# Panel loads out of attention, two panels summed in the first layer, s1 rows in four pieces, value products on VectorE

## What is computed

```python
seq = (x @ W_seq).reshape(2048, 16, 32)
s1, s2 = einsum('nhd,d->hn', seq, a1), einsum('nhd,d->hn', seq, a2)
scores = leaky_relu(s1[:, :, None] + s2[:, None, :], 0.2) + (1 - adj) * -65500.0
hidden = einsum('hij,jhd->ihd', softmax(scores), seq).reshape(2048, 512)
x = layernorm(x + elu(hidden @ W_out + b_out))
A = (adj + adj.T) * 0.5 + I
A = dinv[:, None] * A * dinv[None, :]         # dinv = rowsum(A) ** -0.5
x = layernorm(x + (adj @ A) @ x)               # adj stands for Coefficient2
```

## Time and profile before

| | us |
|---|---|
| runs shown | 787.64, 788.12, 789.85 (median 788.12) |
| the profiled execution, its own time | 786.61 |
| span of its instructions | 784.8 |
| PE busy | 749.7 (96%) |
| DVE busy | 554.7 (71%) |
| ACT busy | 409.9 (52%) |
| POOL busy | 130.1 (17%) |
| mean share of full TensorE clock granted | 0.992 |

### The profile page before, as it was taken

One profiled execution on the slowest core, in us unless ns is written; L12 is line 12 of the kernel. 1 busy time (PEld: TensorE's weight loads), 2 busy tenths in 40 slices (PEclk: granted clock), 3 DMA queues, 4 the chain that ended last, 5 costly groups with the idle time before them and its releaser, 6 DMA issues.

```text
span 784.8 us, 29353 instructions
## 1 busy us (share of the span) xinstructions
PE 749.7 (96%) x13731; PEld 552.4 (70%) x13731; DVE 554.7 (71%) x799; ACT 409.9 (52%) x302; POOL 130.1 (17%) x142
## 2 busy tenths in 40 slices
PE   6999799988999999999999999999999999999997
PEld 2444699988999999999999999444434444444443
DVE  2887899998988999999999983687772211333233
ACT  2874887986977888788897880333321111000000
POOL 0000113012320211101111001364433100000000
PEclk9999799999999999999999999999999999999999
DMA  7992510255313111011110121599119800001111
GB/s 304 413 406 103 235 57 5 84 110 110 56 60 84 58 58 36 26 58 58 58 58 4 58 71 31 97 186 175 54 31 172 119 0 1 18 36 41 41 40 41
DMA packets 17770, 71.65 MB, mean 91 GB/s; under 512 B 2016, under 2 KB 2016, under 8 KB 13408
## 3 DMA queue, kind: packets, MB, share of 16 engines
q1 hardware_dynamic: 13040, 52.99, 17.7%
q0 software_dynamic: 4608, 16.78, 14.1%
HBM read 77.89 MB, written 8.65 MB: 110 GB/s over the span
## 4 chain that ended last, share of the span: by engine, by line
PE 78%; DVE 15%; issue 5%; ACT 1%; DMA 1%; POOL 0%; DVEq 0%; POOLq 0%; SPq 0%; ACTq 0%
PE bank L631 13%; PE bank L534 12%; PE bank L533 12%; PE bank L531 11%; PE bank L618 11%; PE bank L467 7%; PE bank L579 7%; DVE RZ L852 5%; PE bank L587 3%; DVE RG L871 2%; DVE RG L867 2%; DVE RP L816 1%; PE bank L571 1%; DVE MT L892 1%; DMA RZ<-in_L_gnn_W_seq_dram 1%
## 5 line engine op out<-in xcount | busy, mean ns | idle before, releaser
L531 PE MATMUL bank<-RP,RG 128*128 128x66 f16 x4096 | 388.8, 193 | 6.9 <-DVE RG L871 3.6
L534 PE MATMUL bank<-RP,MT 128*128 128x66 f16 x4096 | 388.7, 194 | 3.6 <-issue 3.6
L531 PEld LDWEIGHTS bank<-RP,RG 128*128 128x128 fp8e4 x4096 | 386.3, 98 | 8.3 <-DVE RG L871 3.6
L533 PE MATMUL bank<-RP,RG 128*128 128x66 f16 x4096 | 388.7, 195 | 2.1 <-issue 2.1
L534 PEld LDWEIGHTS bank<-RP,MT 128*128 128x128 fp8e4 x4096 | 386.4, 98 | 3.2 <-issue 3.2
L533 PEld LDWEIGHTS bank<-RP,RG 128*128 128x128 fp8e4 x4096 | 386.4, 97 | 2.7 <-issue 2.7
L689 ACT ACTIVATE RZ<-RZ,TAB 128x2048 int8<-128x2048 f32 x160 | 306.6, 1988 | 15.3 <-DVE RG L867 14.5
L852 DVE TENSOR_SCALAR RZ<-RZ,TAB 128x2048 int8<-128x2048 f32 x96 | 132.3, 1378 | 0.0
L867 DVE TENSOR_TENSOR RG<-RZ,MT 128x512 int32<-128x512 int32 x160 | 121.7, 760 | 0.1
L631 PE MATMUL bank<-RZ,MT 128*128 128x512 f16 x512 | 110.7, 379 | 2.2 <-DVE MT L1023 2.2
L391 POOL TENSOR_TENSOR RP<-SEQ,TAB 128x528 f32<-128x528 f32 x32 | 52.2, 1652 | 331.8 <-DVE RP L818 256.7
(11 more groups left out here) (103 smaller groups left out, 593.2 us busy)
## 6 DMA issues: line engine op xcount, KB each, us to landing
RG<-in_adj_t_dram SPq DMA_DIRECT2D x16, 1024.0 KB, 10.6
RZ<-s_rows_dram SPq DMA_DIRECT2D x16, 1024.0 KB, 5.8
seq_copy_dram<-SEQ SPq DMA_DIRECT2D x1, 4224.0 KB, 14.2
S2Q<-in_adj_p_dram POOLq DMA_DIRECT2D x8, 512.0 KB, 6.3
S2Q<-in_adj_tp_dram POOLq DMA_DIRECT2D x8, 512.0 KB, 11.3
RZ<-in_x_dram SPq DMA_DIRECT2D x16, 256.0 KB, 3.5
RP<-in_adj_p_dram POOLq DMA_DIRECT2D x8, 512.0 KB, 7.1
RP<-in_adj_tp_dram POOLq DMA_DIRECT2D x8, 512.0 KB, 13.8
```

The lines of the kernel that those rows point to most:

```text
L531: mm(pb[bank][:, c:c + 2 * DV], step, high, start=(j == 0 and i % IB == 0), stop=(j == NT - 1), skip_group_check=True)
L533: mm(pb[bank][:, c:c + 2 * DV], step, low, start=False, stop=(j == NT - 1), skip_group_check=True)
L534: last = mm(pb[bank][:, c + DV:c + 3 * DV], mask, edge, start=False, stop=(j == NT - 1), skip_group_check=True)
```

## The change

- POOL loads no panel during attention. `NE = 2`: panels 0 and 1 are loaded once PE has used all but two slots of the last head, and added at once. The others up to 9 are loaded and added in the loop of the first layer, diagonals three iterations behind. `y_part` sums two panels; `y_product` does 14 instead of 12. Panels 10 to 15 are loaded, added and completed one y_product at a time.
- `NS = 4`: a row of s1 is loaded in four pieces, each behind another quarter of the G tiles of the head before; the readers wait for all four. SP's loop over heads is unrolled.
- `prep` moves to DVE, ahead of `low_operands(0)` for head 0 and at j = 4 of head h for head h+1; its wait for `pn_ready` falls.
- `o_product` 0 and 1 do column tiles 0 to 14 first and the last one of both after that. `take_back(t)` goes ahead of `low_z(t)`.

```diff
--- before.py
+++ after.py
@@ -42,6 +42,8 @@
     CLAMP = 20.0
     NG = 16
     NQ = 4
+    NE = 2
+    NS = 4
     NP = 6
     LAG = 5
     NZ = 4
@@ -54,7 +56,7 @@
     ACTZ = [j for j in range(NT) if j not in OWN]
     NA = 4
     GT = 4
-    AT_EVAC, AT_HIGH, AT_LOW, AT_HID = 7, 8, 11, 13
+    AT_PREP, AT_EVAC, AT_HIGH, AT_LOW, AT_HID = 4, 7, 8, 11, 13
     assert CW * IB <= 512 and 2 * NB == 8
     ctx = ExitStack()
@@ -316,21 +318,23 @@
             sp.dma_start(s1_rows[:, :], s1T).then_inc(s1_stored, 16)
             sp.wait_ge(s1_stored, 16)
-            def load_s1(h, u):
-                sp.dma_start(S1B[:, u, :], s1_rows[DS(h, 1), :].broadcast_to([P, N])).then_inc(s1b_in[u], 16)
+            def load_s1(h, q):
+                i = slice(q * (N // NS), (q + 1) * (N // NS))
+                sp.dma_start(S1B[:, h % 2, i], s1_rows[h:h + 1, i].broadcast_to([P, N // NS])).then_inc(s1b_in[h % 2], 16)
             sp.wait_ge(seq_ps, NT)
-            load_s1(0, 0)
-            load_s1(1, 1)
+            for q in range(NS):
+                load_s1(0, q)
+            for q in range(NS):
+                load_s1(1, q)
             sp.wait_ge(tabs_done, 1)
             sp.dma_start(seq_copy[:, :], SEQ[:, :, :, :].rearrange("p t h d -> p (t h d)")).then_inc(seq_stored, 16)
-            with sp.Fori(1, H // 2) as p:
-                for u in range(2):
-                    h = p * 2 + u
-                    sp.wait_ge(z_ready, h * NV - NV)
-                    sp.wait_ge(g_ready, h * NT - NT)
-                    load_s1(h, u)
+            for h in range(2, H):
+                sp.wait_ge(z_ready, (h - 1) * NV)
+                for q in range(NS):
+                    sp.wait_ge(g_ready, (h - 1) * NT + q * (NT // NS))
+                    load_s1(h, q)
             sp.wait_ge(z_ready, (H - 1) * NV)
             sp.wait_ge(g_ready, (H - 1) * NT)
@@ -383,18 +387,6 @@
                 gp.affine_select(out=m[:, :], in_=m[:, :], compare_op=ALU.not_equal, fill=one, base=0,
                                  pattern=[[-1, P]], channel_multiplier=1).then_inc(consts, 1)
-            def prep(h):
-
-                if h >= 1:
-                    gp.wait_ge(pn_ready, h)
-                for e, tab in enumerate((EE, FF)):
-                    gp.tensor_tensor(V2[:, :, e, :], SEQ[:, :, h, :], tab[:, h, :].unsqueeze(2).broadcast_to([P, NT, DV]),
-                                     ALU.mult).then_inc(v2_ready, 1)
-
-            gp.wait_ge(tabs_done, 1)
-            prep(0)
-            prep(1)
-
             gp.wait_ge(deg_done, 1)
             gp.tensor_tensor(DINV[:, :], DINV[:, :], mhalf[:, :], ALU.pow).then_inc(pow_done, 1)
@@ -410,15 +402,6 @@
                 diag = panel(t)[:, t, :]
                 gp.tensor_tensor(diag, diag, id2[:, :], ALU.add).then_inc(s2_done, 1)
-            for h in range(2, H):
-                prep(h)
-                if 3 <= h < 3 + NQ:
-                    load_panel(h - 3)
-                if 4 <= h < 4 + NQ:
-                    add_panel(h - 4)
-                if 5 <= h < 5 + NQ:
-                    add_diagonal(h - 5)
-
             def x_minus_1(t):
                 gp.wait_ge(xr_in[t % 2], (t // 2) * 16 + 16)
                 gp.tensor_tensor(xr[:, t % 2, :], xr[:, t % 2, :], mone[:, :].broadcast_to([P, D]), ALU.add).then_inc(xm_done, 1)
@@ -430,24 +413,32 @@
             x_minus_1(0)
             x_minus_1(1)
+            gp.wait_ge(g_used, NG + H * NT - 2)
+            for t in range(NE):
+                load_panel(t)
+            for t in range(NE):
+                add_panel(t)
             gp.wait_ge(att_end, 1)
             for t in range(NT):
-                if t < NP:
-                    load_panel(NQ + t)
-                if 2 <= t < 2 + NP:
-                    add_panel(NQ + t - 2)
-                if 4 <= t < 4 + NP:
-                    add_diagonal(NQ + t - 4)
+                if t + NE < NQ + NP:
+                    load_panel(t + NE)
+                if NE <= t < NQ + NP:
+                    add_panel(t)
+                if 2 <= t < 2 + NE:
+                    add_diagonal(t - 2)
+                if 3 + NE <= t < 3 + NQ + NP:
+                    add_diagonal(t - 3)
                 rstd_of(t, var_done, rstd_done)
                 if t + 2 < NT:
                     x_minus_1(t + 2)
-            for t in range(NQ + NP, NT):
-                gp.wait_ge(y_ps, NQ if t < 2 * NQ + NP else t - NQ - NP + 1)
-                load_panel(t)
-            for t in range(NQ + NP, NT):
-                add_panel(t)
-            for t in range(NQ + NP, NT):
-                add_diagonal(t)
+            for t in range(NQ + NP, NT + 2):
+                if t < NT:
+                    gp.wait_ge(y_ps, t - NQ - NP + 1)
+                    load_panel(t)
+                if NQ + NP < t <= NT:
+                    add_panel(t - 1)
+                if NQ + NP + 1 < t:
+                    add_diagonal(t - 2)
             for t in range(NT):
                 rstd_of(t, var2_done, rstd2_done)
@@ -582,7 +573,7 @@
             def y_part(j):
                 pe.wait_ge(xl_done, j + 1)
-                for i in range(NQ):
+                for i in range(NE):
                     for l in range(2):
                         last = mm(pb[NQ + i][:, :], S2Q[:, i, j, :], XH[:, l, j, :],
                                   start=(j == 0 and l == 0), stop=(j == NT - 1 and l == 1))
@@ -603,7 +594,7 @@
                 out_product(t, late if t < 2 else every)
                 if t == LAG:
                     pe.wait_ge(banks_free, H)
-                    pe.wait_ge(s2_done, NQ)
+                    pe.wait_ge(s2_done, NE)
                 if t >= LAG:
                     y_part(t - LAG)
             for t in range(NT - LAG, NT):
@@ -619,25 +610,30 @@
                                   start=(j == 0 and l == 0), stop=(j == NT - 1 and l == 1))
                 last.then_inc(y_ps, 1)
-            def o_product(t):
-                if t < 8:
+            def o_product(t, js):
+                if js[0] == 0 and t < 8:
                     pe.wait_ge(yv_done, t + 9)
-                else:
+                elif js[0] == 0:
                     pe.wait_ge(ov_done, t - 7)
-                for j in range(NT):
+                for j in js:
                     if t == 0:
                         pe.wait_ge(yv_done, j + 1)
                     for l in range(2):
                         last = mm(pb[(t + NQ) % 8][:, :], MT8[:, j, t * P:(t + 1) * P], ZH[:, l, j, :],
                                   start=(j == 0 and l == 0), stop=(j == NT - 1 and l == 1))
-                last.then_inc(o2_ps, 1)
+                if js[-1] == NT - 1:
+                    last.then_inc(o2_ps, 1)
             pe.wait_ge(v_added, NT)
-            for t in range(NQ, NT):
+            for t in range(NE, NT):
                 y_product(t)
             pe.wait_ge(mt_back, NT)
-            for t in range(NT):
-                o_product(t)
+            for t in range(2):
+                o_product(t, range(NT - 1))
+            for t in range(2):
+                o_product(t, range(NT - 1, NT))
+            for t in range(2, NT):
+                o_product(t, range(NT))
         @block.scalar
@@ -680,7 +676,7 @@
             def att_head(h):
                 u = h % 2
-                sc.wait_ge(s1b_in[u], (h - u) * 8 + 16)
+                sc.wait_ge(s1b_in[u], (h // 2 + 1) * 16 * NS)
                 for j in range(NT):
                     if j in ACTZ:
                         m = h * NV + ACTZ.index(j)
@@ -809,6 +805,13 @@
             own.wait(ve)
             V.memset(RD[:, :], 1.0).then_inc(tabs_done, 1)
+            def prep(h):
+
+                own.wait(ve)
+                for e, tab in enumerate((EE, FF)):
+                    V.tensor_tensor(V2[:, :, e, :], SEQ[:, :, h, :], tab[:, h, :].unsqueeze(2).broadcast_to([P, NT, DV]),
+                                    ALU.mult).then_inc(v2_ready, 1)
+
             def low_operands(h):
                 u = h % 2
@@ -846,7 +849,7 @@
             def att_head(h):
                 u = h % 2
-                ve.wait_ge(s1b_in[u], (h - u) * 8 + 16)
+                ve.wait_ge(s1b_in[u], (h // 2 + 1) * 16 * NS)
                 def own_step(m):
                     V.tensor_scalar(ZD[:, (h * len(OWN) + m) % 2, :], S1B[:, u, :], S2[:, h, OWN[m]:OWN[m] + 1], -1.0,
@@ -877,6 +880,8 @@
                         add_low_sums(h - 1)
                     if h > 0 and j == AT_EVAC + 3:
                         norms(h - 1)
+                    if j == AT_PREP and h < H - 1:
+                        prep(h + 1)
                     if j == AT_LOW and h < H - 1:
                         low_operands(h + 1)
                     if h > 0 and j == AT_HID:
@@ -891,6 +896,7 @@
                 V.tensor_tensor(MT32[:, j, :], MT32[:, j, :], EMP32, ALU.bitwise_or).then_inc(mt_full, 1)
+            prep(0)
             low_operands(0)
             for k in range(KC):
                 find_empty(k)
```

(2 more changed lines are left out.)

## The result

The changed kernel takes **792.55 us** (median of 10 runs) where the kernel before takes 788.35 beside it (10 runs): a ratio of **1.0048**, with an interval from 1.0037 to 1.006. One of the changed kernel's ten runs was slow (804.61 us; the other nine took 790.91 to 795.31), as was one of the seven of the experiment with the first panels early and four in the loop (2686.89 us), and the ratios leave both out. It is slower by some 4 us, a little more than the 0.3% that can be told from no change. The forecast was 782.8 with a range up to 790.0, so the sign is wrong and the range missed. The profiled execution took 791.06 us with a span of 789.2, against 786.61 and 784.8 before.

The account below looks back on a forecast made before the run. Attention was taken as bound by PE and its pauses. From 786.6 us, -11.2 for attention, +8.0 for the first layer and -2.1 before the o_products gave 781.3; with 1.5 for the median 782.8 us, range 776.5 to 790.

Parts of the forecast that it names:

- Pauses that go with the panels: Attention: 12.6 us lost in PE pauses, taken as waits for code behind data; without panel loads 11.6 us at most goes.
- eight heads without a pause: Attention after 250 us: the 1 MB s1 load alone causes no PE pause in eight heads.
- `prep` on DVE: Attention: costs DVE 1.25 us per head, covered by PE's 24.07; net +0.3 us at matmul 624, otherwise no gain.
- The two collisions on DVE: Attention, head 1: L852 and L867, slowed by POOL's products, lose 1.8 us each time; both go.
- s1 in pieces at no cost: Attention: last piece lands after 3.5 us, at worst 5.8; ACT's next Z comes 1.6 to 3.9 later, covered: 0.
- The first two panels cost nothing: First layer start: asked for 3 us before attention ends, needed 25 us later: 0; late x rows would add 1 to 3.
- Panels 6 to 9 in the loop: First layer: waits for panel landings hold POOL and DVE, so the stretch ends 5 to 7 us earlier instead of 10.1.
- The best case of +3.7: First layer ends 10.1 us earlier, added y_product matmuls cost 13.8: +3.7 us; as a rival, 778.5 us, chance 0.17.
- DVE's slack of 0.8 us in a step of 4.73: First layer loop: DVE needs 3.9 us per step; argument for the loop staying with PE, chance 0.17.
- The gap ahead of the first o_product: Before the first o_product: PE's 2.16 us wait is covered by the new order and 60 matmuls: -2.1 us.
- the price of the exchange: First layer and y_products: two panels fewer in y_part, two more y_products, DMA delays included: +8 us, from +6.8 to +8.6.
- The rule of turns between queues: First layer: DMA engines alternate between software and hardware queues, x rows get half, sum near +4 us; not adopted.

## Why the prediction was wrong, point by point

- **Pauses that go with the panels** (12.6 - 1.0 of excess): that they go with the panels is right and was shown. The size is 9.0 us, not 11.6. I had let one pause of 1.0 us stay; the changed kernel keeps 3.4 us, four pauses of 0.2 to 0.6 us where no panel is loaded, and one of 1.7 where 1.0 had been. (The first dents, too, lie in slices 9 and 10 of PE's row, not in slices 6 to 12.) One of each:

```profile
313.43 0.19 PE L524 MATMUL bank<-RP,RG 128*128 128x66 f16 x1 [0.38 <-issue]
...
452.06 0.20 PE L524 MATMUL bank<-RP,RG 128*128 128x66 f16 x1 [1.55 <-issue]
```

  They are not the work of the small pieces: with whole s1 rows the excess is 3.3. But without s1 rows from head 2 on they are gone between 236 and 455 us, so s1 has a part in them. Which transfer meets which packet of code seems to shift from one kernel to the next, and my "eight heads without a pause" was one such meeting. The row read 114.00 busy of 114; after, it is 113.62. What picks the packets that are late stays open.
- **`prep` on DVE**, +0.3 us at matmul 624: measured +0.28, which is luck. In the ten kernels with `prep` on DVE that matmul starts at 110.9 to 112.4 us, though eight of them are the same up to there. The two collisions on DVE are 1.7 us by its rows, not 1.8. Its cover held, its gift to DVE was worth nothing, both as said.
- **s1 in pieces at no cost**: held, though a piece landed after 3.3 us and ACT does wait for it.
- **"The first two panels cost nothing"** failed. I had named the condition, x rows 2 and 3 late behind them, priced it at 1 to 3 us and left it out of the sum. Moving the two panels away gave 2.9 and 4.3 us in the first layer (2.9 beside eight panels in the loop, 4.3 beside four). The error lies in taking "PE needs them 25 us later" for slack: POOL issued a load, two adds and a second load in one burst, and the x row that DVE needed first had to land beside them.
- **Panels 6 to 9 in the loop**: I priced them at 10.1 - 5.8 = 4.3 us, taking +8 from +3.7 (the upper end of +8.6 should have been 13.8 - 5 = 8.8); taking them out gave 4.6 (5.9 with the first two panels out already). The size is right or somewhat small, the chain only half: panels awaited ahead of `rstd_of` held DVE for 1.56 and 2.23 us, but the waits of 1.58 and 2.52 us were for x rows that had landed late themselves.
- **The best case of +3.7** was not reached even then; it comes to +6.6 there. With both costs away the stretch takes 86.4 us, where 93.6 - 10.1 is 83.5. Of these 2.9 us, 1.3 are one step of 6.0 instead of 4.73, and 1.6 the tail, which I had let end 1.4 us sooner for its shorter backlog of `y_part` and which takes 13.1 us as against 12.9 before. PE's last lines in that kernel, and the stretch behind the first of them:

```profile
566.45 1.89 PE L580 MATMUL bank<-RG,S2Q 128*128 128x512 f16 x4 [3.15 <-DVE RG L997]
569.78 5.56 PE L580 MATMUL bank<-RG,S2Q 128*128 128x512 f16 x16 [1.45 <-DVE RG L997]
...
566.30:573.10 6.80, 5.10 (x12) 1.30 (x12) 6.25 (x15) 1.81 (x3) 2.91 (x4) 0.50 0.00 0
```

  With half the `y_part` work PE now waits 3.15 us for DVE, the clock falls to half, and the 16 matmuls take 5.56 us instead of 3.9. The clock took back what the halved backlog had saved.
- **DVE's slack of 0.8 us in a step of 4.73**, which would have let the loop make good a delay, wasn't there. A step of DVE at the end takes 4.57 us without a wait, and in it one operation takes twice as long beside POOL's `x_minus_1` (565.16 to 566.19):

```profile
564.70 0.68 DVE L981 TENSOR_TENSOR RZ<-bank,W 128x512 f32<-128x512 f32 x1
565.30 1.44 DVE L1009 SCALAR_TENSOR_TENSOR RZ<-RZ 128x512 f32<-128x512 f32 x1
...
569.38 0.69 DVE L1009 SCALAR_TENSOR_TENSOR RZ<-RZ 128x512 f32<-128x512 f32 x1
```

  The 3.9 was 5.60 less a wait of 1.70, and in that longer step the same operation (L1003 there) stood clear of POOL at 0.68. A shorter step brings DVE's and POOL's work on top of each other.
- **The gap ahead of the first o_product**, -2.1: measured -2.3, and it is the gain that the kernel with the panels in attention keeps.

The step that failed is thus the price of the exchange, +8 where 15.5 was measured: the first two panels at nothing, and a best case that took from DVE's long step a slack that the short one doesn't have. The terms close: measured from the best case of 83.5, the changed kernel's 95.3 us are 11.8 more. I had priced 4.3 of them; panels 6 to 9 are 4.6, the first two 4.3, the remainder 2.9. The 7.5 us by which the first layer was missed are 0.3 + 4.3 + 2.9, and attention's 2.5 are the pauses that stayed. The rule of turns between queues, weighed and put aside there, would have been further off still: more x rows landed late than in the kernel before, not fewer.

## What to carry to other kernels

Bulk transfers that seem free beside a busy TensorE can delay its code: look for pauses put down to nothing that are a fixed number of instructions apart, and count them against the transfers before moving either. Before swapping cheap filling of one stage for more work in another, price the bare swap by itself; here it lost 5 to 7 us with most of the transfers out of the way. Where transfers are moved into a stage whose DMA share is already near one, ask which small load that stage waits for first and put them behind that; their own due time says little. And slack read as step less wait is that of the long step: in a shorter one the same operations may collide.

## What the runs showed of the hardware

- TensorE's clock fell to half behind waits of 2 to 3 us in the first layer: behind 2.96 us at 509.43 for 3.4 us, and with waits of 2.03 and 3.53 us around it from 564.3 for 10.2 us. In the kernel before, a wait of 1.43 us there left it at full, and so did one of 1.95 at 551.66 in the changed kernel; a pause of 1.94 at 211.06 in attention, with the panels there, was followed by 3.4 us at half. While it was down, four `y_part` matmuls took 1.60 to 1.89 us instead of 1.03.
- A code packet of 16 KB can start 6.3 to 7.6 us behind the one before it, where 4.0 is regular, when panels are loaded, and now and then beside a 1 MB row of s1 or W_out; its own transfer stays at about 1 us. Cutting the data into DMAs of 128 KB didn't prevent it.
- An x row of 256 KB on SyncE's queue, asked for in the first layer, landed after 2.4 to 3.5 us when no panel was on its way as it was asked for (47 rows of the twelve traces), after 2.9 to 4.9 beside a plain load alone (13 rows), and after 7.4 to 9.3 in 87 of the 108 cases in which an accumulating add was under way as it was asked for; the other 21 took 2.4 to 5.7. That is so with four, six or eight panels in the loop; what differs is how many rows are caught. Whether it is the adding or only the amount that is queued, no run tells.
